# Scaling the late-layer rows of edgeless nodes in the mean and score stages instead of the two convolution stages

## What is computed

```python
x = _layernorm(x + _L0_gnn_ref(x, edge_index, W1, b1, W2, b2))            # two convolutions
x = _layernorm(x + _L1_gnn_ref(x, edge_index, edge_type_8, W, root, bias))# x @ root + bias + mean per relation
x = _layernorm(x + _L2_gnn_ref(x, W_att, edge_index, edge_type_8))        # attention messages only
x = _layernorm(x + _L3_gnn_ref(x, W_sum, edge_index, edge_type_16))       # relu of summed messages only
```

## Time and profile before

| | |
|---|---|
| median of 3 runs | 3763.21 us (3763.13 to 3765.24) |
| the profiled execution | 3760.51 us, of which the span is 3758.6 us |
| TensorE busy | 2909.0 us (77%) |
| VectorE busy | 2965.8 us (79%) |
| ScalarE busy | 1678.5 us (45%) |
| GpSimd busy | 1858.1 us (49%) |
| mean granted TensorE clock | 0.914 |

### The profile page before, as it was taken

One profiled execution on the slowest core, in us unless ns is written; L12 is line 12 of the kernel. 1 busy time (PEld: TensorE's weight loads), 2 busy tenths in 40 slices (PEclk: granted clock), 3 DMA queues, 4 the chain that ended last, 5 costly groups with the idle time before them and its releaser, 6 DMA issues. The chain is left out here.

```text
span 3758.6 us, 57586 instructions
## 1 busy us (share of the span) xinstructions
PE 2909.0 (77%) x10747; PEld 1631.2 (43%) x10747; DVE 2965.8 (79%) x8628; ACT 1678.5 (45%) x4665; POOL 1858.1 (49%) x1779
## 2 busy tenths in 40 slices
PE   2665664666655566799986888877999899999997
PEld 1433443555545555344433444443343344444443
DVE  7886555999969999699983555557999878888886
ACT  2775775888857677455541111113444411111111
POOL 2775776444434443355536777750000046666664
PEclk9998887889878887799998999988999999999998
DMA  2664444555545655233322222222222211111111
GB/s 64 198 194 147 150 150 134 190 198 199 198 139 193 197 185 186 94 92 92 92 82 80 87 88 86 83 61 66 92 92 85 86 49 45 46 50 49 50 53 34
DMA packets 267148, 418.71 MB, mean 111 GB/s; under 512 B 54780, under 2 KB 116537, under 8 KB 267082
## 3 DMA queue, kind: packets, MB, share of 16 engines
q1 hardware_dynamic: 210634, 318.80, 25.9%
q0 software_dynamic: 56448, 99.21, 9.5%
HBM read 215.60 MB, written 206.07 MB: 112 GB/s over the span
## 5 line engine op out<-in xcount | busy, mean ns | idle before, releaser
L1225 PE MATMUL bank<-sum_masked,sum_w 128*128 128x512 f32 x1568 | 691.1, 594 | 1.4 <-DVE sum_masked L1302 1.4
L1112 POOL DMA_INDIRECT sum_rows<-t_x,sum_gi x196 | 228.1, 1164 | 691.8 <-ACT sum_gi L1136 646.7
L1302 DVE SCALAR_TENSOR_TENSOR sum_masked<-sum_typ,sum_col 128x512 f32<-128x512 bf16 x784 | 487.9, 683 | 18.9 <-ACT sum_col L1155 16.9
L1496 POOL DMA_INDIRECT at_rows<-t_x,at_gi x392 | 391.5, 999 | 172.9 <-issue 124.5
L1592 DVE SCALAR_TENSOR_TENSOR at_masked<-at_typ,at_col 128x512 f32<-128x512 bf16 x392 | 247.0, 691 | 260.1 <-ACT at_col L1530 234.6
L1225 PEld LDWEIGHTS bank<-sum_masked,sum_w 128*128 128x128 f32 x1568 | 291.2, 191 | 332.2 <-issue 271.3
L1225 PE MATMUL bank<-mean_masked,mean_w 128*128 128x512 f32 x784 | 377.5, 612 | 18.8 <-DVE mean_masked L1302 18.8
L1225 PE MATMUL bank<-att_masked,att_w 128*128 128x512 f32 x784 | 380.4, 613 | 9.7 <-DVE att_masked L1302 7.7
L1553 PE MATMUL bank<-at_masked,at_ww 128*128 128x512 f32 x784 | 377.7, 627 | 1.9 <-DVE at_masked L1592 1.9
L1112 POOL DMA_INDIRECT mean_rows<-t_x,mean_gi x196 | 224.0, 1143 | 232.8 <-ACT mean_gi L1136 185.4
L1112 POOL DMA_INDIRECT c_rows<-t_g,c_gi x196 | 187.1, 955 | 274.9 <-ACT c_gi L1136 138.3
(11 more groups left out here) (289 smaller groups left out, 5696.2 us busy)
## 6 DMA issues: line engine op xcount, KB each, us to landing
t_x<-c_dense_x SPq DMA_DIRECT2D x196, 256.0 KB, 3.7
pf_xc<-x_dram SPq DMA_DIRECT2D x98, 256.0 KB, 3.0
t_g<-pf_g SPq DMA_DIRECT2D x98, 256.0 KB, 3.1
t_x<-pf_x SPq DMA_DIRECT2D x98, 256.0 KB
c_dense_x<-t_x SPq DMA_DIRECT2D x98, 256.0 KB, 3.8
out_dram<-c_dense_x SPq DMA_DIRECT2D x98, 256.0 KB, 4.0
c_same<-p_same SPq DMA_DIRECT2D x98, 128.0 KB, 3.5
t_g<-c_new SPq DMA_DIRECT2D x49, 256.0 KB
```

Source lines behind the costliest of these rows:

```text
L1112: pool.indirect_dma_start(rows[:, q, j, :], None, source, bass.IndirectOffsetOnAxis(ap=gi[:, q, j:j + 1], axis=0))\
L1225: pe.matmul(H[q][:, :], w[:, r, :], masked[:, r % MASKS, :], start=(r == 0), stop=(r == n_rel - 1))\
L1302: v.scalar_tensor_tensor(out=masked[:, r % MASKS, :], in0=typ[:, q, :], scalar=float(r), in1=col[:, q, :], op0=ALU.is_equal, op1=ALU.mult) ...
L1496: pool.indirect_dma_start(rows[:, q, side, j, :], None, m.tables["X2"], bass.IndirectOffsetOnAxis(ap=gi[:, q, side, j:j + 1], axis=0))\
```

## The change

`fourth` is gone, `second_and_third` makes only the second-layer rows, and one of each three stores stays. `shifts` keeps for every node two ratios (third and fourth scale over second scale) in a new tile `m.ratio`, with one VectorE instruction of 128x8. A new class `LateLayer` runs in MEAN (third layer, to X3) and in the score stage (fourth layer, to OUT): in each of the 49 steps SyncE loads two chunks of second-layer rows (512 KB) from table X2, ScalarE multiplies them with eight instructions of 128x128, and SyncE stores 512 KB.

```diff
-    def second_and_third(self, act, s, q):
+    def second(self, act, s, q):
         if runs(s):
             act.wait_ge(self.shift_ready, s + 1)
-            for i, (rows, stored, ready) in enumerate(((self.x2, self.x2_stored, self.x2_ready),
-                                                       (self.x3, self.x3_stored, self.x3_ready))):
-                if runs(s, 2):
-                    act.wait_ge(stored[q], of_slot(s - 2, q, 16))
-                for j in range(BT):
-                    last = act.activation(rows[:, q, j, :], self.z[:, q, j, :], ACT.Identity,
-                                          bias=self.shift[:, q, i, j:j + 1], scale=self.scale[:, q, i, j:j + 1])
-                last.then_inc(ready, 1)
+            if runs(s, 2):
+                act.wait_ge(self.x2_stored[q], of_slot(s - 2, q, 16))
+            for j in range(BT):
+                last = act.activation(self.x2[:, q, j, :], self.z[:, q, j, :], ACT.Identity,
+                                      bias=self.shift[:, q, j:j + 1], scale=self.scale[:, q, 0, j:j + 1])
+            last.then_inc(self.x2_ready, 1)
...
     def shifts(self, v, s, q):
         if runs(s):
             v.wait_ge(self.scale_ready, s + 1)
...
+            ratio = self.m.ratio[:, :, bass.ds((s * 2 + self.parity) * BT, BT)]
+            v.tensor_tensor(ratio, self.scale[:, q, 1:3], self.sd[:, 0:1, :].to_broadcast([P, 2, BT]), ALU.mult)
+            v.scalar_tensor_tensor(out=self.shift[:, q], in0=self.mv[:, :, 0], scalar=-1.0, in1=self.scale[:, q, 0],
+                                   op0=ALU.mult, op1=ALU.mult).then_inc(self.shift_ready, 1)
...
+class LateLayer:
...
+    def load(self, sp, s, q):
+        if runs(s, 0):
             if runs(s, 2):
...
+                hold(sp, self.ready, s - 1)
+            sp.dma_start(self.x2[:, q], pair_of_chunks(self.m.tables["X2"], s)).then_inc(self.loaded[q], 16)
+
+    def scale(self, act, s, q):
+        if runs(s, 0):
+            act.wait_ge(self.loaded[q], of_slot(s, q, 16))
+            if runs(s, 2):
+                act.wait_ge(self.stored[q], of_slot(s - 2, q, 16))
+            for j in range(2 * BT):
+                last = act.activation(self.x[:, q, j, :], self.x2[:, q, j, :], ACT.Copy,
+                                      scale=self.m.ratio[:, self.layer, bass.ds(s * 2 * BT + j, 1)])
+            last.then_inc(self.ready, 1)
+
+    def store(self, sp, s, q):
+        if runs(s, 0):
+            hold(sp, self.ready, s + 1)
+            sp.dma_start(pair_of_chunks(self.out, s), self.x[:, q]).then_inc(self.stored[q], 16)
...
@@ -1087,7 +1108,10 @@
                 if conv:
                     dense.load(sp, b + 2, q)
-                    dense.stores(sp, b, q)
+                    dense.store(sp, b - 3, 1 - q)
+                if kind == MEAN:
+                    late.load(sp, b + 2, q)
+                    late.store(sp, b - 1, 1 - q)
...
@@ -1153,6 +1179,8 @@
                     act.activation(col[:, o, :], T[o][:, :], ACT.Copy).then_inc(col_ready, 1)
+                if kind == MEAN:
+                    late.scale(act, b, q)
                 s = b - 3
...
@@ -1410,7 +1438,6 @@
                     if kind == CONV2:
                         statistics(b - 2, q)
-                    dense.fourth(v, b - 2, q)
                     if kind == CONV2:
                         normalise(b - 2, q)
...
```

More of the change, by code:

```diff
@@ L855, in __init__ @@
         self.var, self.sd = sb("dense_var", [P, 3, BT]), sb("dense_sd", [P, 3, BT])
[L856 to L861, removed]
+        self.scale, self.shift = sb("dense_scale", [P, 2, 3, BT]), sb("dense_shift", [P, 2, BT])
+        self.loaded, self.x2_stored = (pair("dense_" + n) for n in ("loaded", "x2_stored"))
+        self.turned, self.copied, self.root_done, self.z_ready, self.x2_ready = (
+            sem("dense_" + n) for n in ("turned", "copied", "root_done", "z_ready", "x2_ready"))
         self.stats_ready, self.mv_ready, self.var_step, self.var_ready, self.sd_ready, self.scale_ready, self.shift_ready = (
@@ L870, in load @@
             sp.dma_start(self.x1[:, q], rows_of(self.source, s * 2 + self.parity)).then_inc(self.loaded[q], 16)
-    def store(self, sp, s, q, name, ready, rows, stored):
+    def store(self, sp, s, q):
         if runs(s):
[L874 to L880, removed]
+            hold(sp, self.x2_ready, s + 1)
+            sp.dma_start(rows_of(self.m.tables["X2"], s * 2 + self.parity), self.x2[:, q])\
+                .then_inc(self.x2_stored[q], 16)
     def all_stored(self, sp):
-        for stored in (self.x2_stored, self.x3_stored, self.x4_stored):
-            for q in range(2):
-                hold(sp, stored[q], of_slot(NB - 1 - (NB - 1 - q) % 2, q, 16))
+        for q in range(2):
+            hold(sp, self.x2_stored[q], of_slot(NB - 1 - (NB - 1 - q) % 2, q, 16))
     def turn(self, pe, s, q):
@@ L964, in shifts @@
             v.wait_ge(self.scale_ready, s + 1)
[L965 to L972, removed]
-            if runs(s, 2):
-                v.wait_ge(self.x4_stored[q], of_slot(s - 2, q, 16))
-            for j in range(BT):
-                last = v.tensor_scalar(self.x4[:, q, j, :], self.z[:, q, j, :], self.scale[:, q, 2, j:j + 1],
-                                       self.shift[:, q, 2, j:j + 1], ALU.mult, ALU.add)
-            last.then_inc(self.x4_ready, 1)
+            ratio = self.m.ratio[:, :, bass.ds((s * 2 + self.parity) * BT, BT)]
@@ L1059, in edge_stage @@
             dense = DenseLayers(m, sb, sem, H, 0, m.tables["X1"])
+        if kind == MEAN:
+            late = LateLayer(m, sb, sem, 0, "X3")
         ctx.callback(sem.clear)
@@ L1098, in _ @@
                 dense.all_stored(sp)
+            if kind == MEAN:
+                late.all_stored(sp)
             if kind != SUM:
@@ L1190, in body @@
                 if conv:
-                    dense.second_and_third(act, b - 2, q)
+                    dense.second(act, b - 2, q)
                 s = b - 3
@@ L1459, in attention_stage @@
         LAST = NB - 1
+        late = LateLayer(m, sb, sem, 1, "OUT")
         ctx.callback(sem.clear)
@@ L1712, in build @@
         m.weight_col, m.alpha_col, m.row_col, m.end_col = map(column, ("weight", "alpha", "row", "end"))
[L1713 removed]
+        m.node, m.ratio = sb("node", [P, RPP]), sb("ratio", [P, 2, RPP])
         m.dst_int, m.hi_int, m.lo_int = (sb(n, [P, KT], I32) for n in ("dst_int", "hi_int", "lo_int"))
```

17 lines of the change are left out of this document (13 added, 4 removed).

## The result

The changed kernel takes 3870.86 us (median of 4 runs, 3867.07 to 3875.21) against 3763.17 us before: a ratio of 1.0286, 95% interval 1.0268 to 1.0304. That is 107.7 us slower, where 77 us slower was forecast, inside the range of 3792 to 3898. The profiled execution has a span of 3865.3 us, 106.7 us over that of before.

A forecast was written before the change was run, and what follows sets the result against it. VectorE was taken to bound the convolutions, VectorE with TensorE MEAN, GpSimd the score stage. Convolutions -62, MEAN +133 and +6 for a slower start and TensorE's pauses give +77 us: 3840 us, range 3792 to 3898.

The forecast's parts named there:

- What bounds each stage: VectorE full in CONV1 and CONV2, VectorE and TensorE pacing each other in MEAN, GpSimd's gathers in the score stage.
- CONV1: First convolution stage: dropping `fourth` for a small ratio instruction gains 46 us, less 4 for ScalarE's loop: 42 us.
- CONV2: Second convolution stage: without `fourth` the reciprocal waits for ScalarE's root, so 0.42 us a step is gained, 20 us.
- MEAN, first loop: In MEAN, scalings ahead of the root delay VectorE's reciprocal by 2.25 us, making the step 10.8 us instead of 8.54.
- MEAN, second loop: In MEAN, scalings wait for an earlier store to free their tile: 6.46 us plus landing time, 11.36 us a step.
- 3.9 + 0.93 = 4.8, and some gathers beside it; I take 4.9: Landing time of MEAN's 512 KB store in us: alone, plus the load still in its way; taken as 4.9.
- The upper bound of 6.4: Longest landing time put for MEAN's store, in us: load, types, flags and gathers all ahead of it.
- The signs of being wrong: In MEAN: reciprocal's wait under 1.3 us, a store landing after more than 6 us, or a clock below 0.88.
- A store lands after more than 6 us: One of the signs that would refute the forecast, which took 4.9 us for the landing of MEAN's store.
- the second rival: TensorE's clock falls in MEAN to CONV2's 0.78, stretching its loop to 12.5 us: +54 us, 3894 us; chance 0.09.
- the first rival: MEAN's scalings are hidden in ScalarE's idle time, so the kernel gets faster: 3707 us; chance 0.07.
- The score stage: Scalings fit into ScalarE's 4.14 us of idle time while GpSimd sets the pace; +3 us for a slower start.

The follow-up runs named there:

- e7: Kernel before without VectorE's four fourth-layer instructions and their store, ScalarE's eight row instructions kept: 3974.61 us against 4019.01 us, ratio 0.9897.
- e8: Kernel before without ScalarE's four third-layer instructions and their store, VectorE's fourth-layer instructions kept: 4022.46 us against 4029.96 us, ratio 0.9986.
- e1: Changed kernel with MEAN's store of scaled rows moved to the head of SyncE's step: 3809.9 us, ratio 1.013 to the kernel before.
- e2: Changed kernel with MEAN's eight scalings behind the copy of the new rows, not ahead of the root: 3790.02 us, ratio 1.0075.
- e11c: Third run of the e11 kernel, on a chip where the kernel before takes 3761.4 us: 3691.26 us, ratio 0.9816.
- e11: Changed kernel, MEAN's scalings ahead of the turned rows' copy, both stores ahead of the 512 KB load: 3983.37 us against 4019.01 us, ratio 0.9895.
- e10: As e2, with MEAN's store of new rows ahead of the 512 KB load and store: 3981.17 us against 4019.01 us, ratio 0.99.

## Why the prediction was right, and where it was off

*What bounds each stage* was right, and so was the stage by stage reading. The whole span has VectorE at 79% before and 75% after, and this tells nothing of what happened.

*CONV1*, 46 us less 4 forecast, 42.2 measured in 48 steps. That both engines' share was needed is shown by e7 and e8; the prediction had ScalarE as next in line but put it at 4 us in the 46. Had the third-layer instructions stayed, it would have taken over half of the gain.

*CONV2*, 20 us forecast, 25.7 measured, with the predicted wait of the reciprocal for the root (0.36 us a step). The reciprocal moved up by 0.92 - 0.36 = 0.56 us against the statistics, where the prediction had 0.51; the rest of the difference isn't resolved.

*MEAN, first loop*: the scalings' place ahead of the root, 2.35 us long and not covered. Right: with the second loop removed (e1) the step is 10.99 us, where the sum had 10.8, and the reciprocal waits 108.8 us in the stage, 2.3 us a step, where the sum had 2.25.

*MEAN, second loop*: its mechanism is right, the size of one term is not. The failed step is "3.9 + 0.93 = 4.8, and some gathers beside it; I take 4.9": the store lands after 6.0 us (median). With it the loop is 6.46 + 6.0 = 12.46 us, and the 45 steps behind the first three take 12.56 us on average. What went wrong in it can be narrowed down. In e2 the same pair of transfers, with gathers beside it but without the types and flags right ahead, landed after 4.0 and 4.7 us, which is the sum's 3.9 and 4.8. In the changed kernel the types and the flags are issued 1.2 and 0.6 us ahead of the load; there the load took 5.4 us and the store 6.0, and the flags themselves 4.7 us instead of 3.1. So the term put at nearly nothing is what SyncE issues right ahead of the pair. By the prediction's own rate these 256 KB are 0.77 us, which makes 5.6 us (an estimate); the rest isn't resolved, and no run moves the types and flags alone. The upper bound of 6.4, all neighbours in the way, was the better guess. By the 6.15 us for 1 MB that the Trainium skill gives (DMA: Bandwidth & Descriptors, Bandwidth) the prediction had an estimate of 5.5 us for the store and 162 us for MEAN, nearer to the measured 6.0 and 178.3 us than the sum from the rows; where the pair went without types and flags ahead (e2, 4.7 us) it was too high.

*The signs of being wrong.* The reciprocal waits 3.0 us a step (140.8 us in all) where some 2 us were named, and the scalings wait 29.2 us in all for the store, 0.6 us a step where 0.5 was named. "A store lands after more than 6 us" was met to its edge (6.0 us). So the prediction stood close to where it called itself wrong.

*The total* missed by 30 us (106.7 us against 77) only because other misses made up for part of MEAN's 42: CONV2 gained 5.7 us more than forecast, the stretch ahead of CONV1 5.0 and the score stage 3.2, neither of the last two with a reason in the prediction. That part is luck.

*The clock*, the second rival: it fell to 0.89 in MEAN, where the prediction had named 0.88 as the limit. It did not decide: e1, with the store moved and nothing done about the clock, took 61 us off, the second loop has no TensorE instruction in it, and e11c has a granted clock of 1.00. The Trainium skill (TensorE: Matmul & The Clock Gate, HAM oscillation) tells of a kernel that fell back to half clock at each wait. The trace agrees in part: from 1500 us on, the four instructions of masks 6 and 7 took 1.98 or 1.99 us, the time at full clock, in 17 of 44 steps, and 2.5 to 3.8 us in the others. A mean clock of 0.89 is the lower level for about a fifth of the time.

*The scalings are hidden in MEAN too*, the first rival: false for the place that they had, and true for another place on the same engine (e11), where ScalarE was idle. e2 shows that another place on ScalarE, behind the new rows, was not enough by itself: the order of SyncE's queue had to change too (e10). The place ahead of the copy was run only together with the new order. The prediction counted the new stores and loads as waiting, and did not ask who waits behind them on SyncE.

*The score stage*: nothing lost, as forecast, on this chip. The store landed late (the scalings waited 84 us in all for it, in 38 steps), and the step stayed at 10.5 us.

What stays open: why the stretch ahead of CONV1 and the score stage are a few us shorter in the changed kernel, how much of the late landing each neighbour of the store makes, and why the prefill and score stages are slower on two of the chips.

## What to carry to other kernels

Work moved onto an engine that is half idle cost nothing here only where it stood in the idle part; an engine's program order decides this, so look at what stands right behind the new instructions and how much cover that has (here 0.1 us ahead of the root, 3.46 us ahead of the copy). Each double-buffered store closes a loop: issue, landing, reuse, next issue. Put the small stores that free tiles ahead of long loads in the queue, and when you estimate a landing time, count every transfer that is issued shortly ahead (here 4.7 us in e2 and 6.0 us in the changed kernel for the same store).

## What the runs showed of the hardware that was not expected

- A 512 KB load with a 512 KB store 0.6 us behind landed after 5.4 and 6.0 us with two loads of 128 KB right ahead, at a DMA share of 0.45, and after 4.0 and 4.7 us without these right ahead, at a share of 0.54 (e2). One alone took 3.9 us. So the share of the stage didn't tell how long a transfer would take. With the types, the flags and a 256 KB store ahead (e11c, share 0.68), the load took 5.9 and the store 6.8 us.
- After a pause of 3.65 us TensorE took 3.45 us, at a granted clock of 0.57, for four instructions that took 1.98 us at 1.00 in the step before.
- The same kernel takes 3763 us on one chip and 4019 to 4030 us on two others. CONV1, CONV2 and MEAN run at the same step on all (within 0.1 us); CONV1's first rows come at 648 us in e11c and at 805 and 813 us in the two other runs of that kernel, and the score stage's step is 10.6 us against 12.8 and 13.1 us.
